# Softmax of the two self-attentions: exponentials taken per head from PSUM with a bias, in place of subtraction and one wide exponential

## The reference, cut to what matters

```python
scores = jnp.einsum('bhqd,bhkd->bhqk', q, k) * 8 ** -0.5
scores = jnp.where(causal[None, None], -jnp.inf, scores)   # at0 only
attn = jax.nn.softmax(scores, axis=-1)
attn_out = jnp.einsum('bhqk,bhkd->bhqd', attn, v)
```

## Time and profile before

| What | Value |
|---|---|
| Median of 3 runs (lowest, highest) | 3573.45 us (3572.79, 3582.72) |
| Span of the profiled execution, from its first to its last instruction; no other time is listed for it | 3580.4 us |
| `at0`: first scores to last exponential | 41 to 392 us |
| `at1`: first scores to last exponential | 851 to 1174 us |
| Busy over the whole span: PE, DVE, ACT, POOL | 74%, 75%, 45%, 37% |
| Exponentials (line 454) | 256 instructions, 159.5 us |
| Subtractions (line 520) | 256 instructions, 176.9 us |

### The profile page before, as it was taken

One profiled execution on the slowest core, in us unless ns is written; L12 is line 12 of the kernel. 1 busy time (PEld: TensorE's weight loads), 2 busy tenths in 40 slices (PEclk: granted clock), 3 DMA queues, 4 the chain that ended last, 5 costly groups with the idle time before them and its releaser, 6 DMA issues. The chain is left out here.

```text
span 3580.4 us, 45746 instructions
## 1 busy us (share of the span) xinstructions
PE 2661.7 (74%) x14571; PEld 1648.0 (46%) x14571; DVE 2697.9 (75%) x4249; ACT 1605.5 (45%) x2660; POOL 1314.8 (37%) x1031
## 2 busy tenths in 40 slices
PE   5999758885888689996777777787777676565523
PEld 3777547774777455553223333232323222454203
DVE  4666547884676355553899999999999998588688
ACT  4777425554777222223544445444544443222260
POOL 4444235553222000000355555555555556233000
PEclk9999878997999799997888889888889879777766
DMA  1000000000000100001000000000000000100000
GB/s 35 1 0 0 8 29 17 15 8 4 1 0 0 40 1 0 0 0 30 3 0 3 1 3 3 0 3 0 3 0 0 0 0 0 33 12 6 7 0 24
DMA packets 40131, 25.79 MB, mean 7 GB/s; under 512 B 8416, under 2 KB 36720, under 8 KB 39920
## 3 DMA queue, kind: packets, MB, share of 16 engines
q1 hardware_dynamic: 40048, 24.74, 2.4%
HBM read 16.34 MB, written 2.10 MB: 5 GB/s over the span
## 5 line engine op out<-in xcount | busy, mean ns | idle before, releaser
L1819 POOL TENSOR_TENSOR mam_h<-mam_h,mam_c_all 128x1024 f32<-128x1024 f32 x256 | 638.5, 2494 | 556.9 <-DVE mam_h L1901 548.5
L1901 DVE TENSOR_TENSOR_SCAN mam_h<-mam_decay,mam_ps_b 128x1024 f32<-128x1024 f32 x256 | 585.4, 2287 | 10.4
L1559 PE MATMUL mam_ps_y<-mam_h,all_ident 128*128 128x512 f32 x1024 | 570.1, 685 | 6.9 <-DVE mam_y L1873 3.9
L1553 PE MATMUL mam_ps_b<-mam_parts,mam_pick 96*128 96x512 bf16 x512 | 179.2, 437 | 290.2 <-DVE mam_h L1901 290.1
L1718 ACT ACTIVATE mam_decay<-mam_delta,mam_a_neg 128x508 f32<-128x508 f32 x512 | 337.2, 714 | 61.2 <-DVE mam_h L1901 57.1
L1559 PEld LDWEIGHTS mam_ps_y<-mam_h,all_ident 128*128 128x128 f32 x1024 | 219.8, 219 | 265.4 <-issue 231.1
L518 DVE TENSOR_REDUCE at_top<-at_ps_s 128x4 f32<-128x512 f32 x256 | 174.6, 682 | 204.3 <-PE at_ps_s L359 204.3
L1896 DVE TENSOR_TENSOR mam_ps_b<-mam_ps_b,mam_du 128x1024 f32<-128x1024 f32 x256 | 311.3, 1216 | 20.9 <-PE mam_ps_b L1553 13.7
L1710 ACT COPY mam_c_all<-mam_ps_t 128x512 f32<-128x512 f32 x256 | 136.8, 585 | 352.0 <-PE mam_ps_t L1547 352.0
L1553 PEld LDWEIGHTS mam_ps_b<-mam_parts,mam_pick 96*128 96x128 bf16 x512 | 42.0, 104 | 497.4 <-DVE mam_h L1901 422.7
L385 PE MATMUL at_ps_o<-at_probT,at_v_wide 128*128 128x128 f32 x2048 | 244.3, 278 | 4.3 <-ACT at_probT L436 4.3
(11 more groups left out here) (346 smaller groups left out, 5421.7 us busy)
## 6 DMA issues: line engine op xcount, KB each, us to landing
all_x_all<-in_x SPq DMA_DIRECT2D x8, 256.0 KB, 4.5
ret_xg<-all_x_all SPq DMA_DIRECT2D x32, 64.0 KB, 1.8
ret_ctx<-in_ctx SPq DMA_DIRECT2D x32, 64.0 KB, 1.9
mam_xg<-all_x_all SPq DMA_DIRECT2D x8, 256.0 KB, 2.3
xat_xg<-all_x_all SPq DMA_DIRECT2D x8, 256.0 KB, 2.4
xat_ctx<-in_ctx SPq DMA_DIRECT2D x8, 256.0 KB, 2.8
out<-qua_res SPq DMA_DIRECT2D x8, 256.0 KB, 2.3
ret_decay<-in_decay SPq DMA_DIRECT2D x1, 1024.0 KB, 5.7
```

The source lines that it names most:

```text
L1553: last = nc.tensor.matmul(ps_b[:, slot, n, :], pick[:, (s // DT) * C2 + n, :], parts[:, d, :], start=True, stop=True)
L1559: last = nc.tensor.matmul(ps_y[:, s % DT, :], c.ident[:], h[:, s % SLOTS, n, :], start=(s < DT and n == 0), stop=(s >= S - DT and n == C2 ...
L1819: nc.gpsimd.tensor_tensor(h[:, slot, :, :], h[:, slot, :, :], c_all[:, chunk, :, :], ALU.mult).then_inc(hc_ready, 1)
L1901: nc.vector.tensor_tensor_scan(h[:, s % SLOTS, :, :].rearrange("p n t -> p (n t)"), decay[:, s % SLOTS, :, :, :].rearrange("p n g t -> p ( ...
```

## The change

DVE takes the maximum as before, and then multiplies the four maxima of each row by -8^-0.5 into a new small tile, `minus_top`. ACT reads the scores from PSUM itself and computes exp(8^-0.5 * score + minus_top). The bias is one value for each partition and instruction, and each head has its own, so there are four exponentials of 128x128 for a bank where there was one of 128x512. PE's `scores` of the next batch now waits for the exponentials of the last (`exp_ready`).

```diff
@@ attention, tiles and semaphores @@
+        minus_top = m.sb("minus_top", [T, 2, NJ, NK])
-        shifted = m.sem("shifted")
+        top_ready = m.sem("top_ready")
@@ PE: scores @@
                 if exists(i, b - 1):
-                    pe.wait_ge(shifted, (i * G + b) * NJ)
+                    pe.wait_ge(exp_ready, (i * G + b) * NJ)
@@ ACT: step @@
                         for k in ((j - 1, j) if j == NJ - 1 else (j - 1,)):
-                            act.wait_ge(shifted, (i * G + b) * NJ + k + 1)
-                            nc.scalar.activation(prob[:, b % 2, k, :, :], prob[:, b % 2, k, :, :], ACT.Exp, scale=HD ** -0.5).then_inc(exp_ready, 1)
+                            act.wait_ge(top_ready, (i * G + b) * NJ + k + 1)
+                            for head in range(NK):
+                                last = nc.scalar.activation(prob[:, b % 2, k, head, :], ps_s[:, k, head, :], ACT.Exp,
+                                                            bias=minus_top[:, b % 2, k, head:head + 1], scale=HD ** -0.5)
+                            last.then_inc(exp_ready, 1)
@@ DVE: shift @@
                     steps.then(nc.vector.tensor_reduce(top[:, b % 2, j, :], src, AX_X, ALU.max))
                     steps.settle()
-                    nc.vector.tensor_tensor(prob[:, b % 2, j, :, :], src, spread(top[:, b % 2, j, :], T), ALU.subtract)\
-                        .then_inc(shifted, 1)
+                    nc.vector.tensor_scalar(minus_top[:, b % 2, j, :], top[:, b % 2, j, :], -HD ** -0.5, None, ALU.mult).then_inc(top_ready, 1)
```

## The result

The changed kernel takes 3676.2 us (median of 4 runs, 3673.06 to 3692.77) against 3573.12 us (4 runs, 3572.34 to 3582.72): a ratio of 1.0293, 95% interval 1.0263 to 1.0323. It is slower by 103 us, where 63 were forecast, and it lies 4 us above the upper end of the range.

What follows compares the result with a forecast made beforehand. One ring through ACT's and PE's queues was taken to bound each attention step, with PE nearly full; 31 x 1.00 plus 31 x 1.04 us gave +63 us on the 3573.45 us median, so 3637 us, range 3608 to 3672.

Steps and rivals of the forecast that it cites:

- the range: Total time from 3608 us (pitch 0.20 us) to 3672 us (0.31 us, small delay of `scores`), leaving out rivals at both ends.
- the ring: Chain setting an attention step, through ACT from copy 0 to copy 3, then PE: 11.20 us in `at0`, 10.27 in `at1`.
- the sum: Both attentions: 31 steps at 1.00 us in `at0`, 31 at 1.04 in `at1`, together +63 us, giving 3637 us.
- the place between the copies: ACT's gapless stretch from copy 0 to copy 3, holding exponentials of banks 0 and 1; cost there lengthens a step 1.00 us.
- the pitch: What each new biased exponential adds to ACT's queue: 0.257 us, a bank of four 1.03 us against 0.53 before.
- the row of the Mamba pair: Two ACT exponentials with per-partition scale, 1.31 us together, second starting 0.11 us before the first ends; source of the overlap.
- nothing from DVE: DVE's 133 us less work over 64 attention steps brings no time back, since DVE is not in the ring.
- Absorbed: Rival: ACT's idle time in each attention step takes the added work, time stays at 3573 us or 3568; chance 5%.
- DVE in the ring: Rival: DVE held the attention steps, so part of its 133 us comes back, time below 3562 us; chance 3%.
- the dearer bias: Rival: each biased exponential on ACT adds 0.294 us instead of 0.257, 19 us over 62 steps, 3655 us; chance 12%.
- no overlap: Rival: the four exponentials on ACT do not overlap, 0.94 us more a bank, 136 us in all, 3710 us; chance 5%.
- the clock falls: Rival: PE's two longer waits, about 0.9 us, bring 1.2 GHz; `values` alone 3.8 us more in such steps; chance 3%.

Runs made afterwards that it cites:

- mixed kernel: Banks 0 and 1 as in the kernel before, banks 2 and 3 as in the changed kernel: 3577.43 us, ratio 0.9996.
- kernels with the early exponentials: Changed kernel, exponentials of banks 0 and 1 issued ahead of copy 0: 3578.52 us; kernel before, bank 0 ahead of copy 0, banks 1 to 3 behind `kT`: 3528.02 us.
- kernel with one wide exponential: Changed kernel with one 128x512 exponential a bank from PSUM, no bias, maximum not subtracted: 3578.24 us, ratio 0.999.
- padded one: Kernel before with an unread 128x512 ScalarE copy ahead of each exponential of banks 0 and 1: 3683.91 us, ratio 1.030.
- filled kernel: Changed kernel with three extra unread matmuls ahead of each of the two `turn_parts` groups in a step: 3643.26 us, ratio 1.0185.

## Why the prediction was right in the ring and wrong in the sum

*Right: the ring, and where in it the cost falls.* Steps at full clock are 12.24 and 11.37 us, forecast 12.2 and 11.3. The ring's part of the loss is 69 us, forecast 63: `at0` lost 1.03 us a step and not 1.00, `at1` 1.10 and not 1.04, which is 66 us in 62 steps; the rest lies in the first and last steps of the stages. The mixed kernel shows that banks 2 and 3 are free in `at0`'s steady steps and cost 0.07 us in `at1`'s, and the kernels with the early exponentials that it is the place between the copies that costs.

*Right in the number, partly by luck: the pitch,* which is the time from the start of one instruction to that of the next. A group of four adds 1.01 us, an instruction 0.2525 us, against 0.257 from the row of the Mamba pair. The pitch of 294 ns, an estimate from the prices in the Trainium skill ("ScalarE: Activation LUTs", What ACT_TABLE_LOAD costs), is not borne out by this trace. The length of one, though, is 442 ns in the mean and not 367:

```profile
L456 ACT ACTIVATE at_prob<-at_ps_s,at_minus_top 128x128 f32<-128x128 f32 x1024 | 295.8, 442 | 1.4 <-DVE at_minus_top L524 1.4
```

So the length was 0.075 us more than forecast and the overlap 0.19 us and not 0.11, 0.08 us more. The two errors cancel, which nothing in the forecast's working made sure of; only their difference, the pitch, enters the sum.

*Right: nothing from DVE.* It lost 2697.9 - 2585.1 = 113 us of work (133 forecast; the small multiplication takes 228 ns and not 170, which is 15 of the 20 us between them), and the kernel with one wide exponential shows that this is worth nothing. Absorbed, DVE in the ring, the dearer bias and no overlap all fall.

*Wrong: "the clock falls".* It stood as a rival with a chance of 3% "in the upper tail", and the sum was made at a clock of 1.00. It is the case that came, and its size is 24 us in `at0` and 8 in `at1`, 32 together; 69 + 32 is the 101 us of the attentions. The step that failed is the one that dismissed it from the earlier trace rows: at the end of `at0` PE waits 1.38 us once and keeps a clock of 1.00. That was one stretch of a few steps, and the same trace has a second one, which the forecast did not read. At the end of `at1`, in the kernel before, PE waits the same 1.38 us in the same place, and the clock falls:

```profile
1172.64 5.44 PE L385 MATMUL at_ps_o<-at_probT,at_v_wide 128*128 128x128 f32 x32 [1.38 <-ACT at_probT L436]
```

```profile
1173.00:1176.40 3.40, 3.40 (x18) 3.40 (x18) 1.11 (x2) 1.11 (x2) 0.00 (x0) 0.50 0.00 0
```

`values` takes 5.44 us there and not 3.81. So the trace of before held both outcomes of one wait, and the price of the bad one, 1.63 us. Besides, the ends of a stage have one such wait in a step, and the changed kernel has two, of 0.87 and 0.90 us, in every one of some 30 steps.

The runs in a row: two waits of 0.35 and 0.38 us, of 0.55 and 0.58, and one of 0.90 go with 1.00 in `at0`; two of 0.87 and 0.90 go with 0.93, in the changed kernel and in the padded one; the same two filled with idle work go with 1.00. The forecast's own price was more than twice too high as well: it put `values` at 3.8 us more in such a step, where the whole slow step costs 1.63 us, since only a part of it runs at 1.2 GHz: `values` took 5.10 us instead of 3.79, and the second `turn_parts` ahead of it, at 215.56, 0.98 us instead of 0.62.

The Trainium skill ("TensorE: Matmul & The Clock Gate", A second HAM failure mode: psum-queue depth-cycling) describes a like pattern in another kernel, with wider bf16 matmuls: it cycles through its PSUM banks, TensorE is idle for short times between its groups of matmuls, and its clock swings between the two levels. The trace agrees, with 0.88 as the mean clock of a slow step beside 1.00 in its neighbour. Whether it is the length of a wait, their number or their sum in a step that counts, these runs don't separate. One kernel that keeps the clock has a single wait as long (0.90 us), another has two that are shorter (0.55 and 0.58 us), and both have a smaller sum.

*The range* ended at 3672 us because it held the uncertainty of the pitch, which turned out to be small, and nothing of the clock, which was the larger one. With the clock at 1.00, as in the filled kernel, the time is 3643 us, within it.

## What to carry to other kernels

Find the stretch of an engine's queue without a gap, between a release that another engine waits for and the next; an operation there costs its full pitch, and the same operation where the engine waits costs nothing as long as it fits into the wait, so move work before replacing it. Where a trace shows one case of what a rival fears, look for every other case of it before dismissing the rival. When a change lengthens the waits of a TensorE that is nearly full, the loss has a second part: price the same steps with a part at 1.2 GHz and give it a real chance, all the more where the waits recur in every step. Filling the idle time with matmuls that nobody reads tells the two parts apart in one run.

## What the runs showed of the hardware that was not expected

- Six useless matmuls in a step made a kernel 33 us faster (3643 against 3676 us), by the granted clock alone.
- One wait of TensorE of 1.38 us, at the end of `at0` and of `at1` in one execution, was followed by a granted clock of 1.00 and of 0.50.
- Biased exponentials of 128x128 overlap more when they are longer: 0.36 to 0.53 us each (0.44 in the mean), and a pitch of 0.25 to 0.27 us throughout.
- Reading PSUM instead of SBUF did not shorten the length of the wide exponential here, 661 ns without a bias against 658, but it did shorten its pitch, 0.49 us against 0.53. The length in a trace is not what an instruction adds to a queue:

```profile
L455 ACT ACTIVATE at_prob<-at_ps_s 128x512 f32<-128x512 f32 x256 | 156.0, 661 | 1.6 <-DVE at_minus_top L521 1.6
```

- A multiplication of 128x4 on DVE took 0.17 us in most places and up to 0.55 in others. ScalarE's exponentials beside it are not the reason by themselves: in `at1` it takes 0.17 us under a group of four, with POOL idle. All 49 of the 256 that took over 0.25 us ran beside an operation of POOL, in `at0` the third of the four in nearly every step; 120 others beside POOL took 0.25 us or less, so what of it delays DVE wasn't found.

```profile
226.22 1.16 ACT L456 ACTIVATE at_prob<-at_ps_s,at_minus_top 128x128 f32<-128x128 f32 x4
226.64 0.73 POOL L500 TENSOR_TENSOR at_qk<-at_raw,at_cos 128x256 f32<-128x256 f32 x1
226.85 0.54 DVE L524 TENSOR_SCALAR at_minus_top<-at_top 128x4 f32<-128x4 f32 x1
...
1062.41 1.16 ACT L456 ACTIVATE at_prob<-at_ps_s,at_minus_top 128x128 f32<-128x128 f32 x4
1062.91 0.17 DVE L524 TENSOR_SCALAR at_minus_top<-at_top 128x4 f32<-128x4 f32 x1
```
